# One batch's layer norm and gate: z ahead of the norm, folded squares, fused gating

## What is computed

```python
xz = einsum('bchw,oc->bohw', x, in_proj_w)     # x: group-normed input
xx, z = split(xz, 2, axis=1)                   # 192 channels each
z1 = gelu(z)
# xx: depthwise 3x3 conv + gelu, x_proj, four selective scans, summed to y (192 x 2304)
mu = y.mean(-1); var = ((y - mu) ** 2).mean(-1)
y = (y - mu) / sqrt(var + 1e-05) * ln_w + ln_b
y = y * z1
x = x + einsum('bdhw,cd->bchw', y, out_proj_w)
# then group norm, qkv (96 -> 3 x 96), depthwise 3x3 conv, attention, projection, residual
```

## Time and profile before

| | us |
|---|---|
| median of three runs | 10277.98 |
| lowest, highest | 10254.69, 10307.78 |
| the profiled execution | 10287.01 |
| its span | 10285.2 |

### The profile page before, as it was taken

One profiled execution on the slowest core, in us unless ns is written; L12 is line 12 of the kernel. 1 busy time (PEld: TensorE's weight loads), 2 busy tenths in 40 slices (PEclk: granted clock), 3 DMA queues, 4 the chain that ended last, 5 costly groups with the idle time before them and its releaser, 6 DMA issues.

```text
span 10285.2 us, 176575 instructions
## 1 busy us (share of the span) xinstructions
PE 7907.0 (77%) x54832; PEld 2574.0 (25%) x54832; DVE 7526.2 (73%) x6480; ACT 6467.1 (63%) x11834; POOL 6297.6 (61%) x4443
## 2 busy tenths in 40 slices
PE   5576668887788877888788886888878874888658
PEld 2122222222222222222222222222222221222212
DVE  1688758886788867887588867888578876889630
ACT  2343348774577746776477755777467763877468
POOL 0577637774587746776377745777368773777320
PEclk7565579988898988888798988889889885999789
DMA  2556525654356525665156543555255551565200
GB/s 62 161 178 197 179 68 186 192 181 122 126 187 188 185 71 181 190 187 176 63 186 189 187 127 122 182 187 186 77 169 188 181 182 51 187 192 178 86 26 20
DMA packets 768722, 1537.26 MB, mean 149 GB/s; under 512 B 85528, under 2 KB 412996, under 8 KB 758800
## 3 DMA queue, kind: packets, MB, share of 16 engines
q1 hardware_dynamic: 767760, 1525.52, 47.5%
HBM read 1272.74 MB, written 252.44 MB: 148 GB/s over the span
## 4 chain that ended last, share of the span: by engine, by line
PE 37%; issue 18%; DVE 14%; DMA 11%; ACT 10%; POOL 5%; SPq 4%; ACTq 0%; DVEq 0%; POOLq 0%
PE ps L1842 7%; PE ps L1774 6%; DMA job_u<-u_scratch 6%; PE ps L1762 5%; PE ps L1710 4%; ACT probs_buf L1226 4%; DVE rings L1440 4%; DVE ps L1419 3%; DVE job_buf L1440 3%; PE ps L1749 2%; POOL hc_buf L993 2%; PE ps L1942 1%; PE ps L1943 1%; PE ps L1791 1%; ACT rings L1213 1%
## 5 line engine op out<-in xcount | busy, mean ns | idle before, releaser
L1226 ACT ACTIVATE probs_buf<-ps 128x384 f32<-128x384 f32 x6912 | 3146.4, 491 | 1197.9 <-PE ps L1842 1131.1
L993 POOL TENSOR_TENSOR hc_buf<-rings,rep 128x768 f32<-128x768 f32 x1152 | 2091.4, 1815 | 1207.1 <-DVE rings L1440 793.6
L1842 PE MATMUL ps<-qp_buf,kp_buf 108*128 108x384 bf16 x6912 | 2289.8, 352 | 605.0 <-ACT probs_buf L1226 274.4
L993 POOL TENSOR_TENSOR hc_buf<-job_buf,rep 128x768 f32<-128x768 f32 x1152 | 2092.0, 1816 | 994.2 <-DVE job_buf L1440 989.0
L1419 DVE TENSOR_TENSOR ps<-ps,rep 128x768 f32<-128x768 f32 x2304 | 2177.3, 945 | 525.4 <-PE ps L1750 420.2
L1774 PE MATMUL ps<-probs_buf,v_buf 128*13 128x384 f32 x13824 | 1584.7, 533 | 77.7 <-DVE att_buf L1458 46.6
L1762 PE MATMUL ps<-hc_buf,sum_states 128*32 128x144 f32 x24576 | 1508.1, 333 | 144.0 <-POOL hc_buf L993 110.3
L1749 PE MATMUL ps<-st_buf,pick_channel 96*128 96x512 bf16 x2304 | 1011.3, 439 | 601.4 <-DVE rings L1440 232.4
L1440 DVE TENSOR_TENSOR_SCAN job_buf<-rings,ps 128x768 f32<-128x768 f32 x768 | 1368.7, 1782 | 101.1 <-ACT rings L1213 54.8
L1842 PEld LDWEIGHTS ps<-qp_buf,kp_buf 108*128 108x128 bf16 x6912 | 649.7, 98 | 3090.4 <-ACT probs_buf L1226 2132.9
L1213 ACT ACTIVATE st_buf<-st_buf,a_cols 128x768 f32<-128x768 f32 x1152 | 1062.0, 927 | 92.1 <-DMA st_buf<-delta_scratch 91.5
(11 more groups left out here) (190 smaller groups left out, 8297.3 us busy)
## 6 DMA issues: line engine op xcount, KB each, us to landing
st_buf<-delta_scratch SPq DMA_DIRECT2D x1152, 384.0 KB
rings<-delta_scratch SPq DMA_DIRECT2D x1152, 384.0 KB
part_scratch<-job_buf SPq DMA_DIRECT2D x1152, 72.0 KB, 3.3
st_buf<-part_scratch SPq DMA_DIRECT2D x192, 432.0 KB, 7.0
rep<-xd_scratch SPq DMA_DIRECT2D x192, 384.0 KB
job_u<-u_scratch SPq DMA_DIRECT2D x192, 192.0 KB
delta_scratch<-job_buf SPq DMA_DIRECT2D x192, 192.0 KB, 4.8
qp_buf<-qk_scratch SPq DMA_DIRECT2D x864, 36.0 KB
```

What stands on the lines that cost most here:

```text
L993: pool.tensor_tensor(hc[tile % 2][:, chunk(kk, v)], h_ring[t % 2], rep_third(1, kk, v), ALU.mult).then_inc(s["hc_ready"], 1)
L1226: act.activation(probs[(m % 2) * HG + h], bank(slots["score", p]), ACT.Exp, scale=SCALE)\
L1842: pe.matmul(bank(slots["score", p]), k_parts[:, h, m * 128:(m + 1) * 128], q_ring[:, (kk * NS + q) % 2, h, :], start=True, stop=True).then ...
```

## The change

Three edits, all in `back`, and the numbers that follow from them:

1. **z first.** PE's `gates` projects z for all six pieces into banks 5 and 7 and ACT's `gates` takes the gelus into room for all of them in `probs_buf` and `rep` (`zg`), so that none is overwritten. With one bank each, a piece's products wait for the gelus of the piece before (z_act). With a front, `gates` stands inside front chunk 0: on PE between `front_in` of chunk 1 and x_proj of chunk 0, on ACT between the gelus and the table load. Without a front it stands ahead of the wait for y.
2. **One chunk ahead instead of two.** Only front chunk 0 runs ahead of the norm (AHEAD = 1). Chunks 1 to 5 run in the unit part: FRONT_UNITS now puts chunk c behind unit 2 + 3(c-1), so the last is behind units 14 and 15.
3. **Fewer instructions.** DVE adds the squares of the 64-row part onto the first 64 rows (or the other half) of the 128-row part (`ln_sqf`), and the variance is one product instead of two. The gate is two `scalar_tensor_tensor` for each part: (y * ln_w) * rstd, and (y + ln_b) * gelu(z), so four instructions for a piece instead of six.

```diff
-FRONT_UNITS = tuple((3 + 3 * (c - 2) + i, c, part) for c in range(2, NPC) for i, part in enumerate(("gelu", "out")))
-FRONT_SUMS = (4, 7, 10, 13)
+AHEAD = 1
+FRONT_UNITS = tuple((2 + 3 * (c - AHEAD) + i, c, part) for c in range(AHEAD, NPC) for i, part in enumerate(("gelu", "out")))
+FRONT_SUMS = (3, 6, 9, 12, 15)
...
-        zg = [[rep[:, (2 * i + t) * PC:(2 * i + t + 1) * PC] for t in range(2)] for i in range(2)]
+        zg = [probs_buf[:, 0:6 * PC], rep[:, 13 * PC:16 * PC]]
...
+                def gates():
+
+                    for c in range(NPC):
+                        act.wait_ge(s["z_mm"], b * NPC + c + 1)
+                        part, cols = rows(c)
+                        act.activation(zg[0][:, piece(c)], bank(5), ACT.Gelu)
+                        act.activation(zg[1][part, cols], ps[part, 7, 0:PC], ACT.Gelu).then_inc(s["z_act"], 1)
+
                 if fb is not None:
-                    first_chunks(fb, 2)
+                    front_pads(fb, 0)
+                    front_part(fb, 0, "gelu", gates)
+                    front_part(fb, 0, "out")
+                else:
+                    gates()
+                    act.preload_act_table_set(LN_EXP_TABLES)
...
-                for c in range(NPC):
-                    dve.wait_ge(s["ln_mean"], b * NPC + c + 1)
-                    for t, p, x in both(c):
-                        ins = dve.tensor_tensor(x, x, ps[p, c % 2, 0:PC], ALU.subtract)
-                    ins.then_inc(s["ln_cent"], 1)
+                for c in range(NPC + 1):
+                    if c < NPC:
+                        dve.wait_ge(s["ln_mean"], b * NPC + c + 1)
+                        for t, p, x in both(c):
+                            ins = dve.tensor_tensor(x, x, ps[p, c % 2, 0:PC], ALU.subtract)
+                        ins.then_inc(s["ln_cent"], 1)
+                    if c:
+                        part, _ = rows(c - 1)
+                        whole, rest = (x[part, :] for x in sq[(c - 1) % 2])
+                        dve.wait_ge(s["ln_sq"], b * NPC + c)
+                        dve.tensor_tensor(whole, whole, rest, ALU.add).then_inc(s["ln_sqf"], 1)
...
                     for t, p, x in both(c):
-                        ins = dve.tensor_tensor(x, x, rstd[p, piece(c)], ALU.mult)
+                        ins = dve.scalar_tensor_tensor(out=x, in0=x, scalar=ln_w[t][p, :], in1=rstd[p, piece(c)],
+                                                       op0=ALU.mult, op1=ALU.mult)
                     chain.link(ins)
-                    for t, p, x in both(c):
-                        ins = dve.tensor_scalar(x, x, ln_w[t][p, :], ln_b[t][p, :], ALU.mult, ALU.add)
-                    chain.link(ins)
-                    dve.wait_ge(s["z_act"], b * NPC + c + 1)
-                    for t, p, x in both(c):
-                        ins = dve.tensor_tensor(x, x, zg[c % 2][t][p, :], ALU.mult)
+                    part, cols = rows(c)
+                    for (t, p, x), z in zip(both(c), (zg[0][:, piece(c)], zg[1][part, cols])):
+                        ins = dve.scalar_tensor_tensor(out=x, in0=x, scalar=ln_b[t][p, :], in1=z,
+                                                       op0=ALU.add, op1=ALU.mult)
...
-                        pe.wait_ge(s["ln_sq"], b * NPC + c)
+                        pe.wait_ge(s["ln_sqf"], b * NPC + c)
...
-                        over_channels(bank(2 + j), (mean192[:, :], mean192), (sq[j][0], sq[j][1][part, :]), c - 1)\
-                            .then_inc(s["ln_var"], 1)
+                        pe.matmul(bank(2 + j), mean192[:, :], sq[j][0], start=True, stop=True)\
+                          .then_inc(s["ln_var"], 1)
```

More of the change, by code:

```diff
@@ L47 @@
 LN_EXP_TABLES = "natural_log_exp_and_others"
-DVE_CHAIN = 35
+DVE_CHAIN = 29
 PIECES = MB * HG
@@ L1163, in front_part @@
                         .then_inc(s["f_gelu"], 1)
+                    if between is not None:
+                        between()
                     act.preload_act_table_set(LN_EXP_TABLES)
```

65 lines of the change are left out of this document (28 added, 37 removed).

## The result

| | before | after |
|---|---|---|
| median, us (range, runs) | 10275.89 (10251.68 to 10307.78, 20) | 10322.43 (10302.32 to 10347.37, 20) |
| profiled execution, us | 10287.01 | 10318.28 |
| its span, us; mean granted clock | 10285.2; 0.825 | 10316.5; 0.818 |

The ratio is 1.0047, with a 95% interval of 1.0037 to 1.0056: 46.5 us slower, just inside the 0.5% (51 us) that the prediction called "same". Between the two profiled executions it is 31.3 us.

The account below looks back on a forecast made before the run. Engines work hand to hand, the last to end changing by stage, and PE's clock decides. Backs with a front +44.8, without -32.4, unit part +60.6: +73.0 us, 10351 us on the median's scale; range 10255 to 10390.

Parts of the forecast that it names:

- same: Whole kernel: a change within about 0.5% (51 us), which a measurement can't tell from none; chance 0.23.
- main case: Whole kernel: slow clock in all six backs with a front, unit part on the path; 10351 us, chance 0.66.
- a clock that rises in z: Rival, z ahead of the norm: PE reaches 2.4 GHz before the first mean; 10202 us, chance 0.12.
- The first subtraction: Back with a front, from chunk 1's front_in through z and the first mean to DVE's first subtraction: 33.9 us.
- The gate: Gating stage after the norm: bound by PE's slow out_proj, 3.1 us a piece, 21.4 us against 36.2 in batch 1.
- The tail: From the last subtraction to the gate: a fold, two variances and 1.5 us, together 5.2 us.
- The unit part: Stage after the gate: five front chunks instead of four make ACT's first heads square 10.1 us later; +60.6 us, six backs.
- The rival that it is hidden: Unit part: something else ends last behind the units, so the 60.6 us vanish; 10290 us, chance 0.10.
- the norm: First to last subtraction, slow clock: 29.8 us a back, 6.4 a piece, PE's new fold wait eating the saved product.
- Clock rising inside the norm: Rival: the clock rises only in the norm, or in some backs; around 10262 to 10300 us, chance 0.12.
- What follows hangs on that square and moves with it: After the unit part: head norms, transposes and next scans depend on ACT's first heads square, 10.1 us later.
- Trainium skill's rule: TensorE's clock: throttled by default, released by sustained activity, so z or norm would lift it; the prediction held batch 6 against it.

Follow-up runs that it names:

- e1: The changed kernel with front chunk 1 run ahead of the norm again (two chunks ahead, four in the unit part); 10353.11 us, ratio 1.0072.
- e2: The changed kernel without the fold of the squares, so two variance products a piece and no wait of PE for DVE; 10338.07 us, ratio 1.0057.
- e3: The changed kernel plus 15 unread conv products on PE in the wait for chunk 1's input, ahead of z; 10303.65 us, ratio 1.0018.
- e6: The kernel before with only the gate in two instructions added, z still projected piece by piece beside it; 10272.46 us, ratio 0.9987.
- e8: e4 plus 14 unread conv products on PE ahead of the norm in the two backs without a front; 10121.45 us, ratio 0.9846.
- e7: e4 with only front chunk 0 ahead of the norm, as in the changed kernel; 10154.35 us, ratio 0.9880.
- e5: The kernel before with only the folded squares added: one variance product a piece, PE waiting for DVE's fold; 10334.15 us, ratio 1.0050.
- e9: e8 plus six waits and six unread memsets on DVE in each norm, where the fold stood; 10120.43 us, ratio 0.9852.
- e4: The changed kernel with z in the wait for chunk 1's input, two banks in turn, no fold, two chunks ahead; 10145.70 us, ratio 0.9875.
- e10: e8 without each piece's second variance product, leaving the squares of channels 128 to 191 out of the variance; 10088.68 us, ratio 0.9821.

## Why the prediction was nearly right

The prediction said 10351 us and most likely slower by more than 0.5%; measured were 10322, slower by 0.47%. The time lies 3 us below the main case's own range (10325 to 10385) and inside the whole one (10255 to 10390); "same" had 0.23.

**What held.** The slow clock from front_in to the end of the gate in all six backs, but for a piece or two of the norm and of the way into the gate, against the rivals of a clock that rises in z (z's window: 0.50). The first subtraction after 34.1 us (33.9 predicted); steps of 4.07 to 4.20 in z (4.1). The gate 21.6 (21.4), bound by PE's out_proj at 3.1 a piece; DVE's scalar_tensor_tensor step by 0.53 to 0.65 us (0.55), so that a piece is 2.2 to 2.6. The tail 4.8 to 4.9 (5.2). The unit part +60.6 us for six backs, the fifth chunk less the units it displaces; e1 takes it back. The rival that it is hidden is dead.

**The term that was mis-sized: the norm.** I said 29.8 us a back; it is 25.9 to 28.4. The first piece (3.15) and PE's wait for the fold (1.57 to 1.80, I had 1.65) are right. Two things are off. A slow piece takes 6.07 to 6.31 us, not 6.4, since the products behind a wait start 1.42 to 1.44 apart rather than 1.575. And the clock comes up inside the norm for one or two pieces, as in the rows at 2523.79: that piece takes 4.0 us. "Clock rising inside the norm" was a rival, but for the whole of what follows; it rises and falls again. Over six backs with a front the forecast is 17.8 us too long (44.8 less 27.0), over the two others 4.0. By an estimate a third of the 17.8 is the length of a piece and two thirds are the clock: a folded norm that is slow throughout takes 28.9 us, and the six measured ones average 26.9.

**The turn of the loop.** "What follows hangs on that square and moves with it" is not true of PE's first product, which comes 4 us nearer at each of the four turns. It is true of the scans from the third on, and the 17.8 us in the table are no term that the sum lacks. What in the program moves PE's first product is open.

**The sum.** 73.0 less 17.8 and 4.0 is 51.2 us. Between the medians 46.5 were measured (interval 38 to 58), 26.5 less than forecast, so the norm's size alone brings the forecast inside the interval. What makes the change lose is what the prediction named: the unit part's 60.6 us and z's 25 us a back, against the conv that leaves the front and what the gate gives back. The two profiles differ by less, 31.3 us. Of the 19.9 us between, 7.6 are outliers: the heads took 47.5 and 48.5 us in two backs of the profile of before and 43.1 to 43.5 in the others, and after has none of these, while e1, e2, e3 and e6 have such backs too. The other 12.3 lie at the turns, in the scans and in the last row of the table. From the third scan behind a turn to the end of the scans, which no edit touches, the four looped batches together took 3574 to 3615 us in the twelve profiles, so that 12 us between two executions say nothing about the change.

**The rule of the clock.** Of the Trainium skill's rule (TensorE: Matmul & The Clock Gate, Part 1) the prediction said that batch 6 doesn't bear it out for this stream. e2 says so for all eight backs: PE busy for 32.8 of 32.9 us, clock 0.50. e8 gives the other side: conv products brought it up, and the same mean and variance stream then kept it, in both of its backs without a front.

## What to carry to other kernels

Put independent products into a DMA wait that follows a fast stream, not behind the transfer that ends it: the same z cost 25 us a back behind front_in and nothing in the wait (e2: 91.7 us from front_in to the end of the gate; e7: 66.1 to 66.5 where the norm is slow too), and there it carried the clock over in four of six backs (48.0). e2 to e7, with two banks for z as well, is 10338 us to 10154.

Before an operation is taken from the busiest engine at the price of a handover, price the wait with the clock that it may cost: where the norm was fast, the fold saved six products a back and made it 8 to 10 us longer (e5), and where it was slow the fold helped (e2). An instruction merge on one engine gives nothing while another bounds that stage (e6), so ask which engine is left once the other parts of a change are in. And before a shorter wait is booked as a gain, follow it to the next place where the engines meet: PE's 16.8 us at the turn were gone by the third scan.

## What the runs showed of the hardware

- The fp32 products of the norm don't raise TensorE's clock by themselves (0.50 over 32.8 busy us, e2), but keep 2.4 GHz where the conv's brought it (1.00 over 20.1 us, e8). In one norm of 42 behind a conv they lost it with the first product (e9, batch 0). With pauses of 1.6 us in each piece the same products lose it partly when they start fast (0.75, e5) and gain it for a piece or two when they start slow (0.62, after). I had expected only the first sentence of this.
- How long PE idles after a fast stream doesn't alone decide whether the clock falls. Ahead of front_in of chunk 1 (e3, e4, e7 to e10) it was kept after each of the nine idle times up to 1.32 us and lost by the end of front_in after each of the nine from 2.10 us on. Of the twelve from 1.46 to 2.06 us two kept it (1.49 in e7, 2.06 in e3) and ten lost it (1.50 in e7). Ahead of one norm it fell after 0.87 and 0.57 us (e9, batch 0), where the same times kept it in e8.
- With waits of 0.95 us a piece the z products lost a fast clock at the third piece in batch 0 of e3 and at the fifth in batch 2. With one wait of 0.43 us in all six pieces they kept it to their end in batch 1 of e4.
- Six products fewer in PE's program of a back shorten the idle time before its first product of the next batch from 99.0 to 82.2 us over four turns (e8 and e10), six instructions more on DVE leave it (98.4, e9), and the third scan comes no earlier. Why PE's idle time shrinks is open.
